# Attention block on one core: scores and maxima from 12-bit float32r parts in the two row halves of TensorE, projections beside the value batch

## The reference

```python
q = (layernorm(x) @ Wq + bq).reshape(4, 256, 16, 16)     # heads of D = 16
k = (ctx_768 @ Wk + bk).reshape(4, 4096, 16, 16)         # ctx has 192 channels
v = (ctx_768 @ Wv + bv).reshape(4, 4096, 16, 16)
attn = clip(q @ k.T * 16 ** -0.5, -10000, 10000)
x = x + (softmax(attn) @ v) @ Wo + bo                    # float32 accuracy
x = x + causal_self_attention(layernorm(x))              # 256 tokens, 16 heads
x = x + slot_router(layernorm(x))                        # 64 slots, top 8
```

## Time and profile before

| what | value |
|---|---|
| median of 3 runs | 1134.89 us (1134.63 to 1138.36) |
| span of the profiled execution | 1137.6 us |
| PE busy | 1096.2 us, 96% |
| DVE, ACT, POOL busy | 75%, 65%, 39% |
| granted TensorE clock, mean | 0.991 |

### The profile page before, as it was taken

How to read it: one execution, slowest core, us unless ns; L and a number is a source line. 1 busy time by engine, 2 the same in 40 slices (tenths; PEclk the granted TensorE clock), 3 DMA queues, 4 the chain that set the end, 5 groups by cost and what they waited for, 6 DMA issues and landing times.

```text
span 1137.6 us, 52429 instructions
## 1 busy us (share of the span) xinstructions
PE 1096.2 (96%) x22943; PEld 822.4 (72%) x22943; DVE 854.9 (75%) x1603; ACT 739.1 (65%) x1380; POOL 441.2 (39%) x759
## 2 busy tenths in 40 slices
PE   7999999999999999999999999999999998979997
PEld 6676677777777777878777777767778765646655
DVE  4777788888888888888888888879999723783642
ACT  2223777777777777777777777778878875414342
POOL 4456466464555555555555545213000001103220
PEclk9999999999999999999999999999999999998998
DMA  7767545454545445545444454423453010000001
GB/s 202 209 165 177 148 130 137 124 143 132 132 120 139 125 125 137 137 122 135 123 132 125 130 131 120 115 73 80 129 150 102 21 31 3 1 1 2 2 1 37
DMA packets 162884, 120.80 MB, mean 106 GB/s; under 512 B 19891, under 2 KB 161603, under 8 KB 162627
## 3 DMA queue, kind: packets, MB, share of 16 engines
q1 hardware_dynamic: 155619, 110.97, 36.4%
q10 hardware_dynamic: 7008, 6.23, 2.0%
HBM read 88.16 MB, written 28.84 MB: 103 GB/s over the span
## 4 chain that ended last, share of the span: by engine, by line
PE 88%; DVE 5%; ACT 3%; issue 1%; DMA 1%; SPq 0%; POOLq 0%; ACTq 0%
PE st L1529 19%; PE acc L1719 19%; PE mx L1529 18%; PE kps L1529 14%; PE st L1534 2%; DVE kst L1372 2%; PE misc L1529 2%; PE kps L1534 1%; PE mx L1534 1%; PE setB L1977 1%; ACT prob L1000 1%; PE acc L1534 1%; PE st L1891 1%; PE setA L2000 1%; DVE mxp L1115 1%
## 5 line engine op out<-in xcount | busy, mean ns | idle before, releaser
L1115 DVE TENSOR_REDUCE mxp<-mx 128x1 f32<-128x512 f32 x959 | 625.5, 686 | 141.1 <-PE mx L1529 114.0
L905 ACT ACTIVATE prob<-st 128x512 f32<-128x512 f32 x704 | 398.6, 599 | 132.5 <-PE st L1529 130.5
L1529 PE MATMUL st<-qst,kst 99*32 99x256 bf16 x8192 | 431.3, 272 | 1.9 <-ACT prob L905 1.1
L1529 PE MATMUL mx<-kst,qst 96*32 96x512 bf16 x3532 | 376.9, 380 | 1.2 <-DVE mxp L1115 0.2
L1529 PEld LDWEIGHTS st<-qst,kst 99*32 99x32 bf16 x8192 | 279.9, 97 | 85.0 <-ACT prob L905 5.0
L905 ACT ACTIVATE xn<-st 128x512 f32<-128x512 f32 x320 | 185.9, 599 | 61.0 <-PE st L1529 60.2
L1719 PE MATMUL acc<-prob,v_raw 128*17 128x256 f32 x2816 | 189.1, 378 | 1.4 <-ACT prob L905 1.2
L1529 PEld LDWEIGHTS mx<-kst,qst 96*32 96x32 bf16 x3532 | 125.3, 94 | 6.0 <-DVE mxp L1115 5.0
L1719 PEld LDWEIGHTS acc<-prob,v_raw 128*17 128x17 f32 x2816 | 99.0, 97 | 40.2 <-ACT prob L905 1.9
L1529 PE MATMUL kps<-xnT 128*32 128x256 bf16 x2088 | 94.3, 272 | 0.0
L640 POOL CAST xnT<-ctx 128x256 bf16<-128x256 f32 x87 | 34.4, 395 | 137.1 <-DMA ctx<-in_ctxT 84.4
(11 more groups left out here) (429 smaller groups left out, 1303.8 us busy)
## 6 DMA issues: line engine op xcount, KB each, us to landing
kst<-kscr SPq DMA_DIRECT2D x120, 192.0 KB, 3.0
kst<-kscr SPq DMA_DIRECT2D x360, 64.0 KB, 2.9
kscr<-kraw SPq DMA_DIRECT2D x100, 192.0 KB, 2.8
ctx<-in_ctxT SPq DMA_DIRECT2D x93, 128.0 KB, 2.7
ctx<-in_ctxT SPq DMA_DIRECT2D x180, 64.0 KB, 2.6
kscr<-prob SPq DMA_DIRECT2D x16, 192.0 KB, 3.7
kscr<-o_sb SPq DMA_DIRECT2D x12, 192.0 KB, 4.2
qscr<-v_raw SPq DMA_DIRECT2D x8, 192.0 KB, 2.5
```

The source lines that it names most:

```text
L905: act.activation(exps(n), st[n % 3][:, :], ACT.Exp).then_inc(exp_done, 1)
L1115: dve.reduce_max(at, bank_of_max(n)[:, :], AX.X).then_inc(max_red, 1)
L1529: mm = pe.matmul(to[32 * c:32 * c + 32, :], weights[:, 32 * c:32 * c + 32], moving, start=start, stop=stop, skip_group_check=True)
```

## The change

Keys and queries are split into two parts of 12 significant bits (`float32r`, four bytes). A product then contracts 32 rows (first part of the queries with both parts of the keys), 3 rows of shift and 16 rows (second part of the queries with the first of the keys): 51 rows (`HR`). Heads 0 and 2 lie in rows 0 to 50, heads 1 and 3 in rows 64 to 114, so a matmul uses one half of the array's rows and all 128 columns. The quarters of scores and maxima go.

```diff
-                for h in range(2):
-                    at = (8 * q + s // 2) % RB * 512 + (2 * s + h) % 4 * P
-                    mm = quarters(st[n % 3][:, h * T:(h + 1) * T], kst[0:99, j, at:at + P],
-                                  qst[0:99, 4 * (q % 3) + j, :], True, True)
-                mm.then_inc(st_ps, 1)
...
+            def score_half(n, h):
...
+                at = (8 * q + s // 2) % RB * 512 + (2 * s + h) % 4 * P
+                row = slice(64 * (j % 2), 64 * (j % 2) + HR)
+                mm = pe.matmul(st_bank("scores", n)[:, h * T:(h + 1) * T], kst[row, j // 2, at:at + P],
+                               qst[row, 2 * (q % 3) + j // 2, :], start=True, stop=True, skip_group_check=True)
...
-                j, qt, at = m % 8 // 2, m % 2, n // 8 % RB * 512
-                product(bank_of_max(n)[:, :], qst[0:96, 4 * (q % 3) + j, qt * P:(qt + 1) * P],
-                        kst[0:96, j, at:at + 512], True, True).then_inc(max_ps, 1)
+                mx_free(pe, "max", n)
+                j, qt, at = (m + 1) % 4, m % 8 // 4, n // 8 % RB * 512
+                row = slice(64 * (j % 2), 64 * (j % 2) + HR)
+                pe.matmul(bank_of_max(n)[:, :], qst[row, 2 * (q % 3) + j // 2, qt * P:(qt + 1) * P],
+                          kst[row, j // 2, at:at + 512], start=True, stop=True,
+                          skip_group_check=True).then_inc(max_ps, 1)
```

The order of the main loop on PE, with the maximum of the other row half between the two halves of a unit's scores, and the projection half in front of the values:

```diff
-                score_unit(n)
+                score_half(n, 0)
                 if n + AHEAD < NU:
-                    max_unit(quarters, n + AHEAD)
+                    max_unit(n + AHEAD)
+                score_half(n, 1)
                 if t == 1:
-                    spread_low(q, 0)
-                if t == 4:
-                    spread_low(q, 1)
-                if n >= 4 and t % 4 == 2:
-                    values((n - 4) // UQ, (n - 4) % UQ // 4)
-                if t == 8 and q > 0:
-                    finish(q - 1)
-                if t % 8 in (0, 4):
+                    for e in range(2):
+                        spread_low(q, e)
+                if t == 59 and q + 1 < NQ:
+                    turn_shift(q + 1)
+                if t % 8 in (3, 7):
...
+                if n >= 7 and t % 4 == 3:
+                    values((n - 7) // UQ, (n - 7) % UQ // 4)
+                if t == 7 and q > 0:
+                    finish(q - 1)
```

```diff
+        mx_users = []
+        for n in range(NU):
+            q, t = n // UQ, n % UQ
+            if n + AHEAD < NU:
+                mx_users.append(("max", n + AHEAD))
+            if t == 7 and 0 < q < NQ - 1:
+                mx_users.append(("finish", q - 1))
...
+        st_users = []
+        for n in range(NU):
+            q, t = n // UQ, n % UQ
+            st_users.append(("scores", n))
+            if t == 1:
+                st_users += [("low", 2 * q), ("low", 2 * q + 1)]
+            if t == 59 and q + 1 < NQ:
+                st_users.append(("shift", q + 1))
...
+        def st_free(eng, kind, n):
+
+            place = st_place[kind, n] - 3
...
+            if user == "scores":
+                eng.wait_ge(exp_done, m + 1)
+            elif user == "low":
+                eng.wait_ge(low_set, m + 1)
```

In the lead the maxima come in pairs, one in each row half, with two pieces of projection behind a pair:

```diff
-            for n in range(AHEAD):
-                max_unit(whole, n)
-                f = fill(n)
...
+            for n in range(0, AHEAD, 2):
+                max_unit(n)
+                max_unit(n + 1)
+                filling(fill(n))
+                filling(fill(n + 1))
```

```diff
-            def k_rest(c):
...
             def k_split(c):
 
-                pool.wait_ge(k_r, k_steps(c + 1))
-                pool.tensor_copy(parts_of(c)[:, :, 1, :], kres[:, c % 2, :, :]).then_inc(k_2, 1)
-                pool.wait_ge(k_2, c + 1)
-                pool.tensor_tensor(parts_of(c)[:, :, 2, :], kres[:, c % 2, :, :], parts_of(c)[:, :, 1, :],
-                                   ALU.subtract).then_inc(k_3, 1)
+                full, first = parts_of(c)[:, :, 1, :], parts_of(c)[:, :, 0, :]
+                pool.wait_ge(k_full, k_steps(c + 1))
+                pool.tensor_copy(first.bitcast(F32R), full).then_inc(k_1, 1)
+                pool.wait_ge(k_1, c + 1)
+                pool.tensor_tensor(full, full, first, ALU.subtract).then_inc(k_2, 1)
```

More of the change, by code:

```diff
@@ L9 @@
 BF16 = mybir.dt.bfloat16
+F32R = mybir.dt.float32r
 I32 = mybir.dt.int32
@@ L30 @@
 AHEAD = UQ + LD
-NP = 11 * UQ + 48 + AHEAD
+HR = 51
 RB = 12
@@ L793, in k_first_half @@
                     act.wait_ge(*written(c - 2))
[L794 to L795 removed]
+                act.activation(parts_of(c)[:, g, 1, :], kps[:, g * CH:(g + 1) * CH], ACT.Identity,
+                               bias=bk2[:, g:g + 1]).then_inc(k_full, 1)
             def v_copy(bank, c):
@@ L858, in _ @@
             act.wait_ge(q_full, 2)
-            act.activation(q1[:, :, 0:T], q_sb[:, :, 0:T], ACT.Copy).then_inc(q_1, 1)
+            act.activation(q1[:, :, 0:T].bitcast(F32R), q_sb[:, :, 0:T], ACT.Copy).then_inc(q_1, 1)
             k_first(2)
@@ L890, in _ @@
                 k_first(c)
-            for pair in range(2):
-                shift_rows(0, pair)
+            act.wait_ge(rows_set, 8)
+            shift_rows(0)
             k_first(KLEAD - 1)
@@ L1669, in score_unit @@
                 s, j = t // 4, t % 4
-                wait(pe, exp_done, n - 2)
-                if t in (0, 2):
-                    pe.wait_ge(shift_set, 2 * q + t // 2 + 1)
-                for h in range(2):
-                    at = (8 * q + s // 2) % RB * 512 + (2 * s + h) % 4 * P
-                    mm = quarters(st[n % 3][:, h * T:(h + 1) * T], kst[0:99, j, at:at + P],
-                                  qst[0:99, 4 * (q % 3) + j, :], True, True)
-                mm.then_inc(st_ps, 1)
-            def turn_shift(q, pair):
-                if pair == 0:
-                    pe.wait_ge(m_3, q + 1)
-                    wait(pe, head_out, 2 * (q - 1))
-                    wait(pe, low_set, 2 * q)
-                else:
-                    pe.wait_ge(shift_set, 2 * q + 1)
-                    pe.wait_ge(flag_abs, q + 1)
-                for jj in range(2):
+                if h == 0:
+                    st_free(pe, "scores", n)
+                    if t == 0:
+                        pe.wait_ge(shift_set, 2 * q + 2)
@@ new lines, in score_half, with turn_shift @@
+                at = (8 * q + s // 2) % RB * 512 + (2 * s + h) % 4 * P
+                row = slice(64 * (j % 2), 64 * (j % 2) + HR)
+                mm = pe.matmul(st_bank("scores", n)[:, h * T:(h + 1) * T], kst[row, j // 2, at:at + P],
+                               qst[row, 2 * (q % 3) + j // 2, :], start=True, stop=True, skip_group_check=True)
+                if h:
+                    mm.then_inc(st_ps, 1)
+            def turn_shift(q):
+                pe.wait_ge(m_3, q + 1)
+                if q:
+                    st_free(pe, "shift", q)
+                for i in range(2):
@@ L1689, in turn_shift @@
                     for qt in range(QT):
-                        mm = quarters(misc[:, (2 * jj + qt) * P:(2 * jj + qt + 1) * P], spad[:, 2 * pair + jj, qt, :],
-                                      identb[:, :], True, True)
+                        for c in ((0, 1, 3) if i + qt == 0 else (1, 3)):
+                            mm = pe.matmul(shift_bank(q)[32 * c:32 * c + 32, (2 * i + qt) * P:(2 * i + qt + 1) * P],
+                                           spad_rows[:, qt, i * P + 32 * c:i * P + 32 * c + 32], identb[:, :], start=True, stop=True,
+                                           skip_group_check=True)
```

379 lines of the change are left out of this document (189 added, 190 removed).

## The result

The changed kernel takes 1257.6 us (1244.58 to 1266.27, 4 runs) against 1134.79 (1134.63 to 1138.36, 4 runs): a ratio of 1.1042, 95% interval 1.0979 to 1.1105. The ratio leaves out the slowest of the four runs, 1266.27 us, whose mean granted clock is 0.944 against 0.966 in the fastest, and that slowest run is also the profiled execution. The kernel is slower, as forecast, but by 123 us where 60 were forecast, and outside the range of 1105 to 1245. The profiled execution has a span of 1264.5 us, 126.9 more than before.

A forecast was written before the change was run, and what follows sets the result against it. PE's time was taken to bound the kernel (96% busy). Blocks with projections 31, blocks 11 to 14 10, last block 8 and lead 11 add 60 us to the median 1134.9: about 1195 us, range 1165 to 1225 (outer range 1105 to 1245).

The forecast's parts named there:

- the lead: Work ahead of the first scores: a maximum pair goes from 0.43 to 0.62 us, plus late second banks; together 11 us slower.
- the eleven blocks with projections: Middle blocks: each 58.6 us against 55.8, so 11 x 2.8 = 31 us slower.
- The gain: Score units: maxima lie beside score halves, a unit costs 0.22 us instead of 0.44, saving 0.88 in four units.
- The change of tile shape: Between units and projections or values: 0.12 us there and 0.20 back, 0.32 for every four units; bounds 0 and above 0.4.
- The rings of three banks: Four units together: the fourth waits for the first's bank, ending at 1.49 us, not 0.88; group 3.44 against 3.39.
- The small steps: Lower bounds, `finish` and `turn_shift` now stand in the rings: 3.6 us a block, 1.3 before.
- The start: Ahead of the first maximum: some 3 us more memsets against shorter splits, counted even, between 2 better and 3 worse.
- Blocks 11 to 14: Late blocks without projections: each 46.5 us against 44.0, so 4 x 2.5 = 10 us slower.
- the last: Last block, scores, values and router's early products: more shape changes and a group of 2.6 us against 2.2; together 8 slower.
- The signs: Profile after: PE share below 85%, PE waits once in four units, 0.1 us gaps, 190 ns weight loads, blocks 58 to 59.
- first rival: Score and maximum weights load quickly, like bf16: group 3.25 us, middle block 55.6, time about 1147; chance 0.20.
- second rival: Banks come back before the fourth unit: group 2.83 us, block 48.9, time 1070 (1070 to 1130); chance 0.14.

The follow-up runs named there:

- same_half: Changed kernel, but the maximum between two score halves is of the head in the same row half as those scores: 1368.5 us, ratio 1.2060.
- split: Changed kernel with the projection half behind units 1 and 5 of eight and values behind 3 and 7, so two units stand together: 1188.3 us, ratio 1.0455.
- keep_busy: Changed kernel plus 24 bf16 identity products on PE in the idle time ahead of the first maximum: 1229.1 us, ratio 1.0835.
- lead_whole: Changed kernel with the 76 maxima ahead of the first scores made from the bf16 identity on the whole array, idle time kept: 1226.7 us, ratio 1.0809.
- lead_half: Changed kernel with the 76 maxima ahead of the first scores made from the bf16 identity in the same row halves: 1253.6 us, ratio 1.1047.
- best: split_late with DVE's memsets of shrow, spad and qst's zero rows moved behind the first LayerNorm: 1172.1 us, ratio 1.0330.
- push: Changed kernel plus 24 whole-array bf16 identity products behind the third pair of maxima, not ahead of the first: 1244.0 us, ratio 1.0964.
- split_late: Changed kernel with split's order, keep_busy's 24 products, and the value batch in two halves in blocks 12 to 14: 1142.0 us, ratio 1.0047.

## Why the prediction was wrong

Two terms of the sum failed, in like measure: the lead (11 forecast, 42.9 measured) and the eleven blocks with projections (31 forecast, 63.6 measured). Each is 32 us or so of the 67 missed in the profiled execution.

- **The gain: right.** One pass and side by side: a score matmul behind another is 274 to 278 ns long in the group shown above, a maximum some 390 (382 and 504 where they come first behind a change of shape). Bf16 matmuls of the same 256 columns, in `kps`, are 273 long and float32's in `acc` 379. And `same_half` shows the other half of the claim, 3.85 against 3.47 for a group.
- **The change of tile shape: right within its bounds.** 0.355 in `split` for 0.32, with the bound at 0.4.
- **The rings of three banks: right in place, short by a term.** The bare group takes 3.47 (3.44 forecast), a late one 2.70 (2.68). But the forecast put the fourth unit's wait on DVE's bank and had ACT's "a little earlier"; the chain names ACT, whose first exponential starts at 0.57 and not 0.42. The two end almost together. A term is missing, put at nothing without a reason: each second projection half waits for `kps` itself, which ACT copies out behind an exponential. Where it waits, `kps` starts 0.25 us after that copy ends. The chain shows it as `issue`; ACT's instruction, from the view in order of time, stands in the fence behind:

```profile
559.73 0.12 PE misc L1698
559.84 0.19 issue
560.03 0.97 PE kps L1564 x20
```

```profile
559.19 0.59 ACT L879 ACTIVATE v_raw<-kps 128x512 f32<-128x512 f32 x1
```

  With it groups are 3.47, 3.55, 3.47, 3.67: 3.54 in the mean, 0.10 above the forecast's 3.44. That is 1.6 us a block and 18 in eleven blocks, some 12 of it from this wait.
- **The small steps: right.** The four groups that hold them take 4.97, 4.05, 4.64 and 4.40, which is 3.9 above four of 3.54; 3.6 forecast. So a middle block at full clock takes 60.6 where 58.6 were forecast, 22 us in eleven. Late blocks take 46.5, as forecast.
- **Not foreseen in the middle: the clock.** Behind the sparse groups at the start of every second block it drops for 3.4 us, which makes that block 62.2 in place of 60.6. The blocks between are as sparse at their start and mostly keep it. Blocks 0 to 10 take 678.1 us, eleven of 60.6 are 667: some 11 us in all. `split`, whose PE is busy for 10.5 of 11 us there, has no such drop from block 1 to block 10.

```profile
466.00:477.00 11.00, 8.73 (x127) 5.35 (x131) 6.43 (x13) 7.60 (x17) 4.52 (x8) 0.99 0.47 141
477.00:480.00 3.00, 3.00 (x34) 1.53 (x28) 0.69 (x2) 0.53 (x2) 2.65 (x7) 0.50 0.15 42
480.00:526.00 46.00, 41.75 (x621) 26.91 (x623) 33.00 (x61) 31.64 (x63) 23.55 (x43) 1.00 0.41 122
```

- **The lead: the step whose mechanism failed.** "Together 11" counted a pair at 0.62 and the pieces at full clock, with the of a kernel whose clock had come back. At full clock it is right: 9.4 in keep_busy. But at half clock the same work costs 42.9. The forecast had no term for the clock. `lead_whole` against `lead_half`, and `best` with the gap of the kernel before, show that what turned a drop of 3.4 us into one of 82 is the row-half form of the lead's maxima; `keep_busy` and `push` show that the same lead keeps the clock where it has it. That is some 32 us of the 67 missed in this execution.
- **The start: counted even, with 3 us worse as its bound; it is 4.4.** In the other kernels with this start the first maximum came between 35.0 and 37.5 us, so 4.4 is at the low end. It waits for the queries' DMA. `best` shows that DVE's memsets aren't the cause; which of the writes and loads in those queues is, was not tried and stays open.
- Blocks 11 to 14 (10.7 for 10) and the last (7.4 for 8): right.
- **The signs.** Most came as named. PE's share below 85% did not: it is 89%, in the middle too (53.28 of 60 us).
- **Two slips in the working.** The small steps before are 55.8 - 54.2 = 1.6 us a block and not 1.3, which moves one bound only. And the first rival's terms, -2.2 and -2.4 us for its blocks, 7 and 5 for the lead and the last, come to 1142 and not 1147.

The first rival, quick weight loads, falls by the loads' 188 to 192 ns in the mean. That bears on the rule cited for it from the Trainium skill, TensorE: Matmul & The Clock Gate, Weight-path perf modes: float32r counts as FP32 there, so far as these rows tell. The second rival, rings that don't bind, falls by the chain. It was right in a thing it did not say: with two units together they don't bind, and the middle is then faster than before.

What stays open: whether it is the half height of the array, the two instructions at a time or the changes of shape between pairs and pieces that keep the clock from rising in the lead, and why the middle's drops end after 3.4 us all the same. No run had pairs in one row half in the lead, or pairs with pieces of their own shape between them.

## What to carry to other kernels

Before you halve a matmul's time by packing, follow its bank to the engine that empties it and back. That way was 1.23 us here for the first of four, and together with the number of banks it sets how many units may stand together. Interleaving other work behind every second unit cost two more changes of shape, 0.7 us in a group, and won more. And check any stretch behind an idle time for whether its own work can raise the clock again: 2.33 us of idling were followed by 3.4 us at half clock in one form of the program, and by 78.5 in another.

## What the runs showed of the hardware

- PE can be 100% busy and stay at 1.2 GHz: 30.00 of 30.00 us at 0.50, 82 us in all, with float32 whole-array pieces and pairs of matmuls in row halves between them. With bf16 in the same row halves it was 71.7 (`lead_half`), with the pairs on the whole array 6.8 (`lead_whole`). The same work holds 2.4 GHz when it begins there (1.00 in `keep_busy`).
- In `push`, 24 whole-array products without a break had the clock back 2.0 us after the first of them (46.71 to 48.7). In the middle it came back after 3.4 us without any.
- A gap of 0.25 us ahead of the first maximum (`keep_busy`) or of 0.80 (`split_late`) left the clock alone; one of 2.33 did not (`best`, and the kernel before).
- Float32r of 51 rows and 128 columns: one pass, as long as bf16 for 256 moving columns (276 and 273 ns, float32 379), some 390 ns for 512, and a weight load with a median of 185 ns that nothing hides at the first unit of a group.
